# Three-pass output projections, and another order at the front of the last mixture, in a two-layer decoder on Trainium2

## The chip, the cores and the metric

The kernel runs on one core of one Trainium2 chip. The metric is device time in microseconds of one execution. "Before" and "after" mean the kernel without and with the change described below. Line numbers (L2137) are lines of the kernel before.

## The reference

The input x is (4, 512, 256) in float32; ctx has the same shape. Six sublayers follow each other, each as `x = x + sublayer(layernorm(x))`:

```
L0  attn   causal self-attention, 16 heads of 16, q and k scaled by a rope factor, y @ W_proj.T + b_proj
L0  xattn  gelu(x ctx^T) * (x ctx^T), times ctx
L0  ffn    mixture: 8 experts of width 512, top 2 by softmax of the two logits, plus a shared expert
L1  attn   full self-attention, 16 heads of 16, att_v @ W_out.T + b_out
L1  xattn  attention over ctx, softmax over the queries, @ Wo + bo
L1  ffn    mixture: 8 experts of width 1024, top 2, each weight a masked softmax (mask: (m - logit) / max(|logit|, m) > 0.02)
```

The change touches the output projections of both self-attentions and the last sublayer:

```
logits = x @ gate_w.T                    # 2048 tokens, 8 experts
routing_weights, selected = phi_routing(logits)   # two softmaxes over masked logits, one per choice
out += wte[:, e:e+1] * ((silu(x @ w1[e].T) * (x @ w3[e].T)) @ w2[e].T)
```

## The kernel before

Partitions are 128 rows. A batch is 512 tokens, four tiles (`NT`). Five programs run one after the other, with a barrier between them: `attention` for layer 0 (tag l0a: four causal batches), `geglu` (l0g), `moe` for layer 0 (l0m), `attention` for layer 1 (l1a: four self batches, then four cross batches) and `moe` for layer 1 (l1m). In each, a generator writes out one list of steps, and each engine walks that list in order and does the steps it has a part in. So the order of the list is the order of every engine's queue, and semaphores join them.

**Precision.** A plain fp32 matmul on TensorE is two records of the trace for each product. Where the kernel splits both operands into a rounded part (`hi`, float32r, made by ScalarE as a copy) and a rest (`lo`, by a subtraction on VectorE or GpSimd), `three_passes` multiplies hi by hi, lo by hi and hi by lo: three records. Before, the input projections of self batches from the second on and all products of the mixtures were done so; the output projection (`project`, step OUT, L1066 to L1074) was plain fp32.

**Attention.** The list runs in slots: a group of four heads (`g`) has eight slots (`j`), and a slot has scores by key (S), their exponential on ScalarE, in self batches the scores by query of a later group and their row maxima on VectorE (A), and between them the rest of the work. For an out-projection the outputs of two groups are turned back (N: `turn_back` on TensorE into `m_ps`, `copy_back` on ScalarE into `oT`). The projection of a batch comes one batch later: steps OUT at slots 4 and 7 of group 1 in self batches, and at slots 9 and 15 (counted through the batch) of the first cross batch. Each OUT does two token tiles with two halves of the heads each: four products of 128 by 128 by 256. VectorE adds the result to x (ADD). Score buffers form a ring of three. SPLIT rounds the q, k and v weights in the first slots (ScalarE, then GpSimd), XSPLIT does the same for the turned x.

**The mixtures.** Rows are sorted by expert into 23 blocks: 16 of 256 rows and 7 of 128. Each block has one set of weights, w13 in `NF` chunks (512 KB each; `NF` is 2 in l0m, 4 in l1m) and w2 (1 MB in l1m). The steps for block n and chunk f: W or C (w13 of a chunk split, ScalarE then VectorE), G (both hidden products on TensorE, SiLU on ScalarE, product on VectorE), H (hidden rows split), V or CV (w2 split), Y (output product), T (gathered rows turned by TensorE and split). GpSimd gathers the rows of block n + 2 once block n's are turned. In l1m there is one raw w13 buffer and one raw w2 buffer.

**The front of l1m**, in order: LN and TURN per batch; LOGITS; then on VectorE the routing, whose steps each wait for the one before: TOP1, TOP2; RANK (TensorE counts places); EXPERTS (blocks used and, at L2292 to L2299, which expert a block has: `block_expert`, then `experts_known`); ROWS and PLACES (L2341 to L2350, ends with `placed`); HELD (GpSimd writes tile and place of each token, four products, L1864); eight spot rows per step SPOT (VectorE, L2356) and their list products LIST (TensorE). Then UNMASKED 0 and EXP 0 (a masked softmax's differences), LISTS (the row list, `listed`), GATHER, C for chunk 0, UNMASKED 1, EXP 1, SHARES (12 steps for the weights in three parts), WEIGHTS (GpSimd, six products, L1871), TensorE kept warm with 24 idle matmuls, T of block 0, then C for chunk 1 and the first block's G, H and so on. LOAD on SyncE's queue waits for `experts_known` and issues the four chunks of block 0's w13. The space of raw w2 holds half of the spots, so w2 is loaded only after the weight lists (LIST part 2) were made, behind G of chunk 1. The first Y waits for w2's split and for the row weights (WEIGHED).

## Time and profile before

| | us |
|---|---|
| median of 3 runs | 1590.3 (1586.99 to 1592.11) |
| profiled execution | 1590.26 |
| its span, first to last instruction | 1588.5 |
| TensorE busy in the span | 1417.9 (89%) |
| VectorE busy | 1176.2 (74%) |
| ScalarE busy | 908.1 (57%) |
| GpSimd busy | 635.8 (40%) |

The engines are named PE (TensorE; PEld its weight loads), DVE (VectorE), ACT (ScalarE), POOL (GpSimd) and SP (SyncE, which only issues transfers here). The five programs lie at about 0 to 290 us (l0a), 290 to 360 (l0g), 360 to 645 (l0m), 645 to 1156 (l1a, cross batches from about 940 on) and 1156 to the end (l1m). Matmuls overlap, so one lasts longer than the distance to the next. PEclk is the clock granted to TensorE as a share of 2.4 GHz.

### The profile page before, as it was taken

Reading aid. Unit: us, or ns where it says so; the run is one execution under the profiler, and the core shown is the slowest. Engines: PE = TensorE matmul, PEld = TensorE weight load, DVE = VectorE, ACT = ScalarE, POOL = GpSimd, SP = SyncE. Lnnn points to the kernel's source line nnn. Section 1 sums busy time; section 2 is a strip of 40 time slices with the busy share of each in tenths; the row PEclk is TensorE's granted clock in tenths of the full one; section 3 lists DMA queues with packets and bytes.
Section 4 is the critical chain, followed back from the end, with each engine's and each line's share of the span. In section 5 each row is a group of like instructions: output and inputs, shape, how many; then the busy total and the mean of one; then the engine's idle time right before and its main releaser. Section 6 shows DMA issues by size and latency. Waiting matters only on the chain. (4 is left out here: it accounts for less than half of the span.)

```text
span 1588.5 us, 30443 instructions
## 1 busy us (share of the span) xinstructions
PE 1417.9 (89%) x10014; PEld 1000.2 (63%) x10014; DVE 1176.2 (74%) x2501; ACT 908.1 (57%) x1722; POOL 635.8 (40%) x899
## 2 busy tenths in 40 slices
PE   7899998989899999679999999898757899999997
PEld 3455554559899999424444433333245899999997
DVE  4777662554778888378788849998868688888885
ACT  1455553223256666136675678998813577766673
POOL 6565530010225665475554452553314233332221
PEclk8799998998999999869999999999987999999999
DMA  6223210220359887443223331332034687887882
GB/s 172 50 57 62 62 42 16 65 93 34 104 149 255 247 243 210 117 100 61 53 49 55 61 74 42 74 74 64 17 133 136 199 245 240 234 242 230 235 236 68
DMA packets 104571, 194.60 MB, mean 123 GB/s; under 512 B 30465, under 2 KB 55937, under 8 KB 101473
## 3 DMA queue, kind: packets, MB, share of 16 engines
q1 hardware_dynamic: 71760, 154.23, 31.2%
q0 software_dynamic: 31872, 37.79, 13.5%
q8 instruction: 80, 1.31, 0.3%
q10 hardware_dynamic: 784, 0.66, 0.1%
q14 instruction: 75, 0.61, 0.1%
HBM read 135.89 MB, written 18.61 MB: 97 GB/s over the span
## 5 line engine op out<-in xcount | busy, mean ns | idle before, releaser
L878 ACT ACTIVATE l1a_sb_probs<-l1a_s_ps,l1a_sb_kmax 128x512 f32<-128x512 f32 x256 | 172.5, 709 | 18.6 <-DVE l1a_sb_kmax L801 17.7
L766 DVE TENSOR_REDUCE l1a_sb_mx<-l1a_s_ps 128x2 f32<-128x1024 f32 x128 | 153.4, 1218 | 36.5 <-PE l1a_s_ps L982 36.4
L801 DVE TENSOR_REDUCE l1a_sb_kmax<-l1a_s_ps 128x1 f32<-128x512 f32 x256 | 160.5, 677 | 20.4 <-PE l1a_s_ps L1021 19.7
L884 ACT ACTIVATE l1a_sb_probs<-l1a_s_ps 128x1024 f32<-128x1024 f32 x128 | 130.1, 1024 | 72.6 <-PE l1a_s_ps L1021 72.0
L1021 PEld LDWEIGHTS l1a_s_ps<-l1a_sb_qst,l1a_sb_kst 49*128 49x128 f32 (+1 forms) x512 | 48.7, 189 | 163.8 <-issue 87.9
L761 DVE CUSTOM_DVE_ANT_0 l0a_sb_seen<-l0a_s_ps,l0a_sb_above 128x128 f32<-128x128 f32 (+3 forms) x256 | 113.5, 487 | 51.5 <-PE l0a_s_ps L982 51.2
L630 POOL DMA_DIRECT2D l1a_sb_kst<-l1a_sb_hi x228 | 112.8, 498 | 86.7 <-PE l1a_s_ps L1021 80.6
L2137 PE MATMUL l1m_g_ps<-l1m_sb_rows_hi,l1m_sb_hi 128*128 128x256 f32 x512 | 146.8, 287 | 0.4 <-DVE l1m_sb_late L2027 0.4
L2137 PE MATMUL l1m_g_ps<-l1m_sb_rows_lo,l1m_sb_hi 128*128 128x256 f32 x512 | 145.3, 284 | 0.0
L2137 PE MATMUL l1m_g_ps<-l1m_sb_rows_hi,l1m_sb_lo 128*128 128x256 f32 x512 | 145.3, 284 | 0.0
L1021 PE MATMUL l1a_s_ps<-l1a_sb_qst,l1a_sb_kst 49*128 49x512 f32 (+1 forms) x512 | 125.3, 498 | 21.4 <-ACT l1a_sb_probs L878 19.2
L2001 DVE TENSOR_TENSOR l1m_sb_lo<-l1m_sb_raw,l1m_sb_hi 128x512 fp32r<-128x512 f32 x184 | 119.3, 691 | 18.5 <-ACT l1m_sb_hi L1905 17.4
L1845 POOL DMA_INDIRECT out_x<-l1m_sb_late,l1m_sb_add_to x37 | 60.9, 1647 | 174.8 <-DVE l1m_sb_late L2049 165.0
L884 ACT ACTIVATE l0a_sb_probs<-l0a_s_ps 128x1024 f32<-128x1024 f32 (+3 forms) x128 | 88.8, 702 | 60.8 <-PE l0a_s_ps L991 60.3
L2137 PE MATMUL l0m_g_ps<-l0m_sb_rows_hi,l0m_sb_hi 128*128 128x256 f32 x384 | 113.1, 294 | 7.1 <-DVE l0m_sb_rows_lo L1995 6.4
L2137 PE MATMUL l0m_g_ps<-l0m_sb_rows_hi,l0m_sb_lo 128*128 128x256 f32 x384 | 111.1, 289 | 0.0
L2137 PE MATMUL l0m_g_ps<-l0m_sb_rows_lo,l0m_sb_hi 128*128 128x256 f32 x384 | 111.1, 289 | 0.0
L1905 ACT ACTIVATE l1m_sb_hi<-l1m_sb_raw 128x512 fp32r<-128x512 f32 x184 | 104.8, 621 | 0.0
L2137 PEld LDWEIGHTS l1m_g_ps<-l1m_sb_rows_hi,l1m_sb_hi 128*128 128x128 f32 x512 | 98.7, 193 | 1.2 <-issue 0.6
L2137 PEld LDWEIGHTS l1m_g_ps<-l1m_sb_rows_hi,l1m_sb_lo 128*128 128x128 f32 x512 | 98.7, 193 | 0.0
L2137 PEld LDWEIGHTS l1m_g_ps<-l1m_sb_rows_lo,l1m_sb_hi 128*128 128x128 f32 x512 | 98.6, 193 | 0.0
L2137 PE MATMUL l1m_y_ps<-l1m_sb_hi,l1m_sb_h_hi 128*128 128x256 f32 x312 | 90.3, 289 | 8.2 <-DVE l1m_sb_lo L2007 7.2
(437 smaller groups left out, 4011.5 us busy)
## 6 DMA issues: line engine op xcount, KB each, us to landing
l1m_sb_raw<-in_l1m_w SPq DMA_DIRECT2D x92, 512.0 KB, 4.6
l0m_sb_raw<-in_l0m_w SPq DMA_DIRECT2D x72, 512.0 KB, 4.8
l1m_sb_raw<-in_l1m_w SPq DMA_DIRECT2D x23, 1024.0 KB, 6.2
l1a_sb_qst<-l1a_sb_hi SPq DMA_DIRECT2D x256, 32.0 KB, 2.1
l1a_sb_kst<-l1a_sb_hi POOLq DMA_DIRECT2D x228, 32.0 KB, 2.0
l0a_sb_qst<-l0a_sb_hi SPq DMA_DIRECT2D x128, 32.0 KB, 2.2
l1a_sb_qst<-l1a_sb_lo SPq DMA_DIRECT2D x128, 32.0 KB, 2.1
l0a_sb_kst<-l0a_sb_hi POOLq DMA_DIRECT2D x124, 32.0 KB, 2.1
```

The costliest lines, as they stand in the source:

```text
L630: pool.dma_start(in_stack(kst, p, e, n), in_part(source, i, p, e)).then_inc(kstacked[p], 16)
L761: ins = dve.tensor_tensor_reduce(seen[:, j % 2, e, 0:last], buffer("A", b, g, j)[:, e, 0:last], above[:, T - last:T], 1.0, -3e38, ALU.add, ...
L766: dve.tensor_reduce(mx[:, g, qt, 2 * p:2 * p + 2], buffer("A", b, g, j)[:, :, :], AX.X, ALU.max).then_inc(a_max.sem, 1)
L801: dve.tensor_reduce(kmax[:, n % 4, e:e + 1], buffer("S", b, g, j)[:, e, :], AX.X, ALU.max, negate=True).then_inc(kmax_done.sem, 1)
L878: ins = act.activation(probs[:, n % 8, e, :], at[:, e, :], ACT.Exp, bias=kmax[:, n % 4, e:e + 1], accum_out=zsum[:, n % 4, e:e + 1])
L884: act.activation(probs[:, n % 8, :, c0:T], at[:, :, c0:T], ACT.Exp, scale=SCALE).then_inc(exp_done.sem, 1)
L1021: ins = pe.matmul(at[:, e, c0:T], kst[rows, p, kt * P:(kt + 1) * P], qst[rows, p, c0:T], start=True, stop=not causal)
L1845: pool.indirect_dma_start(total, bass.IndirectOffsetOnAxis(ap=at, axis=0), y[:, e % 2, t, :], None, compute_op=ALU.add).then_inc(stored[e ...
L1905: ins = act.activation(two_chunks(hi, s % 2, f), raw13[:, s % n13, f, n, :, :], ACT.Copy)
L2001: ins = dve.tensor_tensor(two_chunks(lo, s % 2, f), raw13[:, s % n13, f, n, :, :], two_chunks(hi, s % 2, f).bitcast(F32), ALU.subtract)
L2137: ins = pe.matmul(at, s, m, start=first and n == 0, stop=final and n == len(passes) - 1)
```

## The change

1. Output projections: in `attention`, `project` uses `three_passes` for the self batches that are not the last batch of the program (`out_parts`: three of l0a, four of l1a). A step OSPLIT comes one slot behind each N: ScalarE rounds `oT` into `o_hi`, GpSimd subtracts into `o_lo`, and `project` waits for it. A fourth SPLIT does the output weights. To make room, `o` takes the rope table's space in l1a and the cross batches' `ox` that of `oT`.
2. Both mixtures: of HELD's four products GpSimd keeps two; ScalarE does the other two as copies with a scale. ScalarE's and VectorE's shares of C and CV become steps of their own (CHI, CVHI).
3. l1m: another order from RANK to the second block. UNMASKED 0 comes right behind RANK, the `block_expert` part of EXPERTS (now BLOCKS) and LOAD behind the spots, SHARES and WEIGHTS behind T of block 0, chunk 1's split ahead of T. Half of the spots lie in x's space (VectorE first waits for the copy of x to memory, `summed`), so w2 is loaded in LOAD, which waits for the first gathered rows after two chunks of w13. w2's split and the second set's chunks move between the first two blocks' steps.

```diff
@@ attention schedule: self_slot and cross_slot (there at j == 7)
-        if first and nxt is not None and j < 3:
+        if first and nxt is not None and j < 4:
             yield "SPLIT", nxt, j, 0
@@
         if j == turn_at and has_last and last[1] % 2:
             yield "N", *last, 0
+        if j == turn_at + 1 and has_last and last[1] % 2:
+            yield "OSPLIT", *last, 0
@@ attention
+            def split_out(b, g, _):                         # GpSimd
+                pair = g // 2
+                if out_parts[b]:
+                    o_round.wait(pool, b, pair)
+                    pool.tensor_tensor(o_lo[:, pair, :], oT[:, pair, :], o_hi[:, pair, :].bitcast(F32), ALU.subtract
+                                       ).then_inc(o_rest.sem, 1)
+            def split_out(b, g, _):                         # ScalarE
+                pair = g // 2
+                if out_parts[b]:
+                    oT_copied.wait(act, b, pair)
+                    act.activation(o_hi[:, pair, :], oT[:, pair, :], ACT.Copy).then_inc(o_round.sem, 1)
@@ project
+                if out_parts[b]:
+                    if b == 0:
+                        pe.wait_ge(w_rest, 4)
+                    o_rest.wait(pe, b, pairs[-1])
...
+                    if out_parts[b]:
+                        ins = three_passes(m_ps[:, (t % 2) * D:(t % 2 + 1) * D],
+                                           [((o_hi[:, pair, rows], o_lo[:, pair, rows]),
+                                             (wout_hi[:, pair, :], wout_lo[:, pair, :])) for pair in pairs])
+                        continue
@@ moe_schedule, layer 1
-        for step in ("TOP1", "TOP2", "RANK", "EXPERTS", "LOAD", "ROWS", "PLACES", "HELD"):
+        for step in ("TOP1", "TOP2", "RANK", "UNMASKED", "EXP", "EXPERTS", "ROWS", "PLACES", "HELD"):
             yield step, 0, 0
         for c in range(NSPOT):
             yield "SPOT", c, 0
             yield "LIST", c, 1
-        yield "UNMASKED", 0, 0
-        yield "EXP", 0, 0
+        yield "BLOCKS", 0, 0
+        yield "LOAD", 0, 0
         yield "LISTS", 0, 0
         yield "GATHER", 0, 0
-        yield "C", 0, 0
         yield "UNMASKED", 1, 0
         yield "EXP", 1, 0
-        yield "SHARES", 0, 0
-        yield "WEIGHTS", 0, 0
+        yield "CHI", 0, 0
+        yield "C", 0, 0
+        yield "CHI", 0, 1
+        yield "C", 0, 1
 
         yield "IDLE", 24, 0
         yield "T", 0, 0
         yield "IDLE", 5, 0
-        yield "C", 0, 1
-
-        between = {1: [("LIST", c, 2) for c in range(NSPOT)] + [("WEIGHED", 0, 0)], nf: [("CV", 0, 0)]}
+        yield "SHARES", 0, 0
+        yield "WEIGHTS", 0, 0
+        yield "CHI", 0, 2
+        yield "C", 0, 2
+
+        between = {2: [("LIST", c, 2) for c in range(NSPOT)], 3: [("WEIGHED", 0, 0)]}
@@ weights_beside
         if nf > 2 and n == 0:
-            return (1, f - 1) if f else (1,)
+            return (1, 1) if f == nf - 1 else (1,)
+        if nf > 2 and n == 1:
+            return ((1, 2), (1, 3), (2, 0, 1), (2, 2, 3))[f]
@@ chunk
-        if nf > 2 and n == 1 and f == 0:
-            yield from prepared(1, nf - 1)
         yield "G", n, f
-        if nf > 2 and n == 0 and f < 2:
-            yield "C", 0, f + 2
+        if nf > 2 and n == 0 and f == 0:
+            yield "CHI", 0, 3
+            yield "C", 0, 3
+        if nf > 2 and n == 0 and 0 < f < 3:
+            for part in (2 * f - 2, 2 * f - 1):
+                yield "CVHI", 0, part
+                yield "CV", 0, part
...
+        if nf > 2 and n == 0 and f == 1:
+            yield from prepared(1, 0)
@@ moe
-                     for t in (raw2[:, 0, :, :].rearrange("p f d -> p (f d)"),
+                     for t in (x[:, 0:NTILE // 2, :].rearrange("p n d -> p (n d)"),
@@ LOAD on SyncE
                 for f in range(NF):
+                    if f == 2 and not shared:
+                        sp.wait_ge(rows_in[0], halves_to(0) * 16)
                     load_w13(s, e, f)
+                if not shared:
+                    load_w2(s, e)
@@ HELD: GpSimd keeps the first part, ScalarE has the second
+            def held_in_tile(*_):
+                act.wait_ge(placed, 1)
+                for k in range(TOP):
+                    act.activation(held[:, k, :, 1, :], own[:, k, :, :], ACT.Copy, scale=const["token"][:, 0:1]
+                                   ).then_inc(in_tile_held, 1)
@@ SPOT on VectorE
+        if c == 0 and phi:
+            dve.wait_ge(sems["summed"], 16)
```

## Rows read from the trace of the kernel before

**Rows 1.** Stages: start:end, length; busy us (records) per engine; clock, DMA share, GB/s.
```profile
985.00:1156.00 171.00, 145.99 (x790) 54.93 (x786) 152.07 (x310) 148.80 (x429) 77.16 (x161) 0.98 0.25 55
1156.00:1239.00 83.00, 49.77 (x448) 39.57 (x448) 63.77 (x196) 24.93 (x46) 23.32 (x27) 0.80 0.46 154
1239.00:1588.00 349.00, 336.65 (x2642) 328.48 (x2642) 274.90 (x446) 226.10 (x420) 99.22 (x69) 0.98 0.73 214
```
**Rows 2.** Waits of PE, 1211 to 1300: total us, times, longest us.
```profile
PE l1m_y_ps L2137 <- DVE l1m_sb_lo L2007: 7.2, 1, 7.2
```
**Rows 3.** Chain of waits, 1200 to 1300: start us, us, what.
```profile
1206.73 4.59 DMA l1m_sb_rows<-xn_dram,l1m_sb_take
...
1213.87 3.69 PE l1m_g_ps L2137 x24
...
1239.29 4.73 PE l1m_y_ps L2137 x24
1244.02 2.88 PE l1m_g_ps L2137 x24
```
**Rows 4.** Timeline of PE at an output step: start us, us, instructions.
```profile
783.09 1.97 PE L1073 MATMUL l1a_m_ps<-l1a_sb_wout,l1a_sb_oT 128*128 128x256 f32 x8
784.98 0.50 PE L1021 MATMUL l1a_s_ps<-l1a_sb_qst,l1a_sb_kst 49*128 49x512 f32 x2
```
**Rows 5.** All waits, 760 to 850: total us, times, longest us.
```profile
ACT l1a_sb_probs L884 <- PE l1a_s_ps L1021: 25.7, 28, 1.7
```
**Rows 6.** Lines L848 and L639: ns min/median/max, first and last start.
```profile
L848 ACT ACTIVATE l1a_sb_x_hi<-l1a_sb_xnT x6: 620/622/641, 705.3 to 831.4; 128x512 fp32r<-128x512 f32 x6
L639 POOL TENSOR_TENSOR l1a_sb_x_lo<-l1a_sb_xnT,l1a_sb_x_hi x6: 1272/1280/1286, 706.0 to 832.1; 128x512 fp32r<-128x512 f32 x6
```
**Rows 7.** Timeline of PE and ACT in the first cross group.
```profile
954.69 1.99 PE L1073 MATMUL l1a_m_ps<-l1a_sb_wout,l1a_sb_oT 128*128 128x256 f32 x8
...
958.09 0.76 ACT L878 ACTIVATE l1a_sb_probs<-l1a_s_ps,l1a_sb_kmax 128x512 f32<-128x512 f32 x1
```
**Rows 8.** Timeline of ACT and PE in layer 0's mixture.
```profile
414.33 0.60 ACT L1931 ACTIVATE l0m_sb_late<-l0m_g_ps 128x512 f32<-128x512 f32 x1 [3.77 <-PE l0m_g_ps L2137]
...
424.67 1.01 PE L2109 MATMUL l0m_t_ps<-l0m_sb_held,l0m_sb_spot 128*128 128x115 bf16 x16 [1.75 <-DVE l0m_sb_spot L2356]
```
**Rows 9.** Timeline of DVE at the front: RANK's wait, BLOCKS, ROWS, UNMASKED 0.
```profile
1182.35 0.17 DVE L2281 COPY l1m_sb_count<-l1m_t_ps 128x8 f32<-128x8 f32 x1 [1.69 <-PE l1m_t_ps L2092]
...
1184.58 0.73 DVE L2293 TENSOR_TENSOR l1m_sb_upto<-l1m_sb_end,const_iota 128x184 f32<-128x184 f32 x2
...
1186.46 0.17 DVE L2328 SCALAR_TENSOR_TENSOR l1m_sb_jump<-l1m_sb_end,l1m_sb_start 128x8 f32<-128x8 f32 x1
...
1201.37 0.28 DVE L2264 SCALAR_TENSOR_TENSOR l1m_sb_ab<-l1m_sb_lg 128x128 f32<-128x128 f32 x1
```
**Rows 10.** Timeline of POOL: the first of four held products.
```profile
1192.80 0.80 POOL L1864 TENSOR_TENSOR l1m_sb_held<-l1m_sb_own,const_iota 128x368 bf16<-128x368 bf16 x1 [25.53 <-DVEq L2349]
```
**Rows 11.** Spots (L2356) on DVE in two stretches: busy us (records), clock, DMA.
```profile
1192.90:1195.90 3.00, 2.98 (x5) 0.50 0.52 213
...
1198.30:1201.40 3.10, 3.10 (x17) 0.50 0.00 0
```
**Rows 12.** Line L1714, 1187 to 1226: time from issue to landing.
```profile
DMA to landing us min/median/max: 3.3/4.0/6.8
```
**Rows 13.** One stage more, with columns as in rows 1.
```profile
1229.00:1233.00 4.00, 3.10 (x27) 2.86 (x25) 2.95 (x5) 3.24 (x7) 0.62 (x1) 1.00 0.91 355
```
**Rows 14.** Timeline of DVE and POOL, 1205 to 1216: splits, SHARES, WEIGHTS.
```profile
1205.49 1.29 DVE L2001 TENSOR_TENSOR l1m_sb_lo<-l1m_sb_raw,l1m_sb_hi 128x512 fp32r<-128x512 f32 x2
...
1209.30 0.29 DVE L2306 TENSOR_TENSOR l1m_sb_df<-l1m_sb_df,l1m_sb_keep 128x128 f32<-128x128 f32 x1 [0.43 <-ACT l1m_sb_l L1888]
...
1212.42 5.51 POOL L1871 TENSOR_TENSOR l1m_sb_held<-l1m_sb_own,l1m_sb_share 128x368 bf16<-128x368 bf16 x6 [2.01 <-DVEq L2320]
...
1213.73 2.01 DVE L2001 TENSOR_TENSOR l1m_sb_lo<-l1m_sb_raw,l1m_sb_hi 128x512 fp32r<-128x512 f32 x2 [0.35 <-ACT l1m_sb_hi L1905]
```

More of the change, by code:

```diff
@@ L359, in attention @@
         probs = sb("probs", [P, 8, 2, T])
-        o = sb("o", [P, T])
+        o = const["rope"] if has_cross else sb("o", [P, T])
         rz = sb("rz", [P, NT, GH])
@@ L400, in attention @@
         w_round, w_rest = sem("w_round"), sem("w_rest")
+        out_parts = [b + 1 < NB and kinds[b] != "cross" for b in range(NB)]
+        o_round, o_rest = (Counts(sem(n), [2 if yes else 0 for yes in out_parts]) for n in ("o_round", "o_rest"))
         hi_done = steps("hi_done", 4)
@@ L1380, in moe_schedule @@
         for f in range(1, nf):
+            yield "CHI", 0, f
             yield "C", 0, f
-        yield "CV", 0, 0
+        for f in range(nf):
+            yield "CVHI", 0, f
+            yield "CV", 0, f
         yield "LN2", 3, 0
@@ L1389, in moe_schedule @@
                    4: [("RANK", 0, 0), ("UNMASKED", 0, 0)],
-                   5: [("EXP", 0, 0), ("EXPERTS", 0, 0), ("LOAD", 0, 0)],
+                   5: [("EXP", 0, 0), ("EXPERTS", 0, 0), ("BLOCKS", 0, 0), ("LOAD", 0, 0)],
                    6: [("SHARES", 0, 0), ("ROWS", 0, 0)],
@@ L1762, in next_w2 @@
                     load_w2(s, e)
-            def first_w2(*_):
-                if not shared:
-                    sp.wait_ge(weights_listed, 1)
-                    load_w2(0, expert(0))
             def second_w13(_, f):
@@ L1774, in second_w13, with second_w2 @@
                     load_w13(1, e, f)
-            def second_w2(*_):
-                if not shared:
+            def second_w2(_, f):
+                if not shared and f == NF - 1:
                     w2_done.wait(sp, 0, NF - 1)
@@ L1860, in held_tokens @@
                 tile_first = const["iota"][:, 32 + 3 * NBLK + 1:].unsqueeze(2).to_broadcast([P, NTILE, NBLK])
-                in_tile = const["token"][:, 0:1].unsqueeze(2).to_broadcast([P, NTILE, NBLK])
                 for k in range(TOP):
-                    for n, part in enumerate((tile_first, in_tile)):
-                        pool.tensor_tensor(held[:, k, :, n, :], own[:, k, :, :], part, ALU.mult).then_inc(tokens_held, 1)
+                    pool.tensor_tensor(held[:, k, :, 0, :], own[:, k, :, :], tile_first, ALU.mult).then_inc(tokens_held, 1)
             def held_weights(*_):
@@ L1913, in split_w2 @@
                                ACT.Copy).then_inc(w2_split.sem, 1)
-            def first_w2(*_):
-                for f in range(NF):
-                    split_w2(0, f)
             def next_w13(n, f):
@@ L1945, in end @@
                                   ).then_inc(const["x_back"][0], 16)
-            run({"END": end, "TURN": turned_rows, "EXP": exp, "T": rows_of, "C": split_w13, "CV": first_w2, "W": next_w13,
+            run({"END": end, "TURN": turned_rows, "HELD": held_in_tile, "EXP": exp, "T": rows_of, "CHI": split_w13, "CVHI": split_w2, "W": next_w13,
                  "V": next_w2, "G": gate, "H": split_h})
@@ L2009, in rest_w2 @@
                                   ).then_inc(w2_done.sem, 1)
-            def first_w2(*_):
-                for f in range(NF):
-                    rest_w2(0, f)
             def next_w13(n, f):
@@ L2058, in end @@
                                   ALU.mult).then_inc(end_read, 1)
-            run({"END": end, "LN1": ln, "LN2": normal, "T": rows_of, "C": rest_w13, "CV": first_w2,
+            run({"END": end, "LN1": ln, "LN2": normal, "T": rows_of, "C": rest_w13, "CV": rest_w2,
                  "W": next_w13, "V": next_w2, "G": hidden, "H": rest_h, "Y": output} | routing)
@@ L2291, in experts, with blocks @@
         then(dve.tensor_tensor(end, start, used, ALU.add))
+    def blocks(*_):
+        end = full("end")
         for k in range(2):
@@ L2382, in row_weights @@
         then(dve.tensor_tensor(full("row_weight"), full("row_weight"), at["row_holds"][:, :, 4, :], ALU.add))
-    return {"TOP1": top1, "TOP2": top2, "UNMASKED": unmasked, "EXPERTS": experts, "SHARES": shares, "ROWS": rows,
+    return {"TOP1": top1, "TOP2": top2, "UNMASKED": unmasked, "EXPERTS": experts, "BLOCKS": blocks, "SHARES": shares, "ROWS": rows,
             "PLACES": places, "SPOT": spot, "LISTS": lists,
```

30 lines of the change are left out of this document (21 added, 9 removed).

## The prediction

> **What bounds the kernel now.** Read first the table of stages [rows 1]. After 1239 TensorE is busy 336.65 of 349 us: it sets the time. It does not in layer 1's cross batches (985 to 1156: VectorE 152.07 and ScalarE 148.80 of 171, a ring of scores, maximum and exponential), and least of all from 1156 to 1239, the front of layer 1's mixture: TensorE 49.77 of 83 us, transfers 0.46. There I went to the waits of TensorE [rows 2]: one of 7.2 us, for VectorE's rest of w2. Third, the chain of waits [rows 3]: the first gathered rows land at 1211.33 (1206.73 + 4.59), the first block's passes stand in the chain from 1213.87, and its output product `Y` only at 1239.29. That product takes 4.73 us where the same 24 records take 2.88 later: after the idle gap it starts at the lower clock. From 1244 to the end the chain is TensorE almost throughout, so an earlier start there moves the end by as much.
>
> **Part A: output projections in three passes.** `out_parts` holds for three batches of layer 0 and four of layer 1, two steps each: 14 steps. A step was four fp32 products, recorded as 8 records, 1.89 us from its start to the next scores [rows 4]; it becomes 12 records, at the 0.120 us spacing of the mixture's three passes (2.88 / 24, [rows 3]) 1.44 us, with the same tail of about 0.19 us 1.63. Each step gives back 0.26 us. Bounds: nothing, where TensorE waits for another engine behind it, and 0.45, without the tail. The six of layer 0 and the first six of layer 1 lie where ScalarE and VectorE wait for TensorE (ScalarE 25.7 us in 28 waits in 90 us of layer 1's self batches, [rows 5]); I take 12 x 0.26 = -3.1.
>
> Added: 14 roundings on ScalarE, 0.62 us each, and 14 subtractions on GpSimd, 1.27 us each, by the same operations on x [rows 6]; one more of each per layer for the weights. In self batches they are queued six or more slots ahead of the product on engines that wait for TensorE there: nothing; if that cover went, a product would wait up to 1.9 us. The weight split falls between the x-bias addition and the splits of x on GpSimd; it pushes the first x rest by no more than its own 1.27 us, with a slot between that and the product that reads it: nothing.
>
> The cross slot is another matter: N is at slot 6, the split at 7, the product at 9. TensorE runs ahead of ScalarE: the product starts at 954.69, three slots before ScalarE's first exponential of slot 10 at 958.09 [rows 7]. Now ScalarE first ends slot 7's two exponentials (at 955.4, two slots of 1.33 us before 958.09), then the rounding (to 956.05), GpSimd the rest to 957.4, and only then TensorE. Behind the product on its queue stand slot 10's scores: 957.45 + 1.5 = 959.0, their maximum by 960.1, so ScalarE's exponential of slot 10 starts near 960.2 where it was 958.09. ScalarE and the ring are the bound here: +2.1 us, of which slack in the ring may absorb some; I take +1.9 (bounds 0.6, the rounding alone, and 3). The second product there (slot 15) hides its gain: 0.
>
> Part A: -3.1 + 1.9 = -1.2. Reusing the rope table and oT as storage adds no wait that isn't there (oT is read out by then through the same `out_ready`).
>
> **Part B: the first mixture (layer 0).** Its order is the same on every engine, except that two of the `held` products move from GpSimd to ScalarE. ScalarE now waits for `placed` in front of the SiLU that starts at 414.33 [rows 8], which VectorE reaches at about the same time; two copies of 368 elements, each below the 0.60 us that 512 take, put that SiLU near 415.4. TensorE has two blocks' products to run meanwhile. GpSimd is done 1.6 us sooner, and TensorE's 1.75 us wait for the first spots (424.67, [rows 8]) shrinks. Between +1 and -1.5; I take -0.5.
>
> **Part C: the front of layer 1's mixture.** Step by step to the gather:
> 1. VectorE waits 1.69 us for `ranked` [rows 9]; UNMASKED (six steps from 1201.37 on, 1.93 us) moves into that wait: +0.25 there.
> 2. BLOCKS (1184.58 to 1186.46, five steps, [rows 9]) leaves that chain: -1.88. It goes behind the spots, where UNMASKED stood, with the same length: 0 there.
> 3. While GpSimd makes `held` (four products of 0.80 us from 1192.80 on, [rows 10]), VectorE gets one spot through per product: 4 or 5 in 3.0 us, against 16 or 17 in 3.1 later [rows 11]. With two products left there, 1.5 us hold two spots and the other two take 0.4: -1.1 (bounds 0 and -2.2).
> So the gather starts 2.7 us sooner, and the rows land at 1208.6 if nothing is in their way.
>
> 4. The weights. LOAD hung on `experts_known` and was issued at 1187.40; now it hangs on BLOCKS, behind the spots: 1203.3 - 2.7 + 1.1 (the same lag from block_expert to issue) = 1201.7. Landings took 3.3 to 6.8, median 4.0 us [rows 12]: chunk 0 at 1205.7, chunk 1 near 1207. CHI and C of both (C 1.29 us each, [rows 14]) fill the gather's wait, done by 1209.3, after UNMASKED 1. First row split, ready at 1210.5: G(0,0) starts at 1210.6 instead of 1213.44, again at the lower clock. Chunks 2 and 3 and w2 wait for the gather and go out from 1208.7. At 512 KB in some 1.5 us (the transfers reached 355 GB/s averaged over 4 us, [rows 13]) they land near 1212.5, 1214 and 1217, set 1's first two near 1220.
> 5. SHARES (1209.30 to 1212.3, 3.0 us, [rows 14]) was free in the gather's wait; now it stands behind the row split, to 1213.6, and GpSimd's six WEIGHTS products (5.51 us) run beside C(0,2), C(0,3) and H(0,0). Two subtractions took 2.01 us instead of 1.29 beside them [rows 14] (0.72 more for the pair, nearly all of it on the second): between 0.36 and 0.72 for each of five or six, I take the upper end, 3.5 us.
> 6. VectorE in the new order then: C(0,2) to 1215.6, SiLU product 1216.3, C(0,3) 1218.9, H(0,0) 1219.8, T1 1220.5, G(0,1) 1221.2, half of w2 1222.4, H(0,1) 1223.0, W(1,0) 1224.3, G(0,2) 1224.9, the other half 1226.1, H(0,2) 1226.7, G(0,3) 1227.3, H(0,3) 1228.6, W(1,1) 1230.2, then the row weights at 1230.5.
> 7. TensorE: G(0,0) 1210.6 to 14.7, T1, G(0,1) to 18.0, G(0,2) to 20.9, the 64 list products to 23.0, G(0,3) to 25.9, G(1,0) to 28.8, T2, and Y(0,0) waits for the row weights: 1230.6. It takes 2.9 us, because the gap before it is 1.3 us and not 7.2. It ends at 1233.5 instead of 1244.02: -10.5. Of this 2.8 comes from the gather, 5.9 from the wait (7.2 to 1.3), 1.8 from the clock.
> 8. In block 1 both chunks W(2,0) and W(2,1) now lie between V and H(1,2): H(1,3) ends some 9.5 us after Y(0,1) instead of 8.5, and Y(1,0) wants it at 8.9: +0.6. After that both orders are the same and TensorE bounds.
> Part C: -9.9; bounds -4 (the first rival below) and -12.
>
> One rule of the Trainium skill (SBUF — State Buffer, Who interferes with whom) speaks against step 5: a VectorE instruction with two SBUF inputs and a GpSimd one that reads SBUF shut each other out for a whole instruction. By it each of six subtractions could lose a full product of 0.8 us, 4.8 in place of 3.5, and the sum would be -10.3; the 2.01 us row shows 0.72 for two of them, so I stay with the row.
>
> **Sum.** -1.2 - 0.5 - 9.9 = -11.6 on the profiled execution's own 1590.26 us (span 1588.5, 1.8 outside it), which equals the median of the runs, 1590.3. Forecast 1579.
>
> **Rivals.**
> *The weights come late (half the gain).* For: the first load moves by 14 us, from an idle stretch into the gather's; 1 MB at 355 GB/s is 3 us in front of the gather's own packets. The Trainium skill (DMA: Bandwidth & Descriptors, Issuing engines are not separate DMA queues) says that all issuers share the same 16 engines; no row here shows a gather beside 1 MB. Against: the gather is issued 0.9 us after the load and its second half 1.4 us later, and its rows are wanted later than the weights. Price: gather +3 and w2 at 1221 instead of 1217, which pushes VectorE's queue by 3: gain 5 to 6, 1585.
> *The wait of 7.2 us only changes its name.* Y(0,0) also waits for the row weights, whose products on GpSimd start at 1213.7 instead of 1212.42 and may be stretched to 1.25 us each, with TensorE's list products in front of G(0,3). If VectorE, locked out, runs 4 us later than in step 6: 1583.
> *Slower: the weight stream becomes the bound.* There are twenty-three sets of 3 MB. If TensorE after 1239 were fed by the stream with no slack, the stream's start 14 us later would reach the end: +14, less 2.8 (gather), less 1.7 (Parts A and B), 1600. It decides once a chunk lands later than its turn in block 1. Against: transfers are busy 0.73 there [rows 1], chunk loads wait for VectorE to free the one raw buffer, and by 1229 the stream owes 3.5 MB, some 12 us of work in 27.
> *No change.* The reordering is absorbed elsewhere and Part A costs what it gives: 1589.
>
> **How the numbers follow.** Forecast 0.68 (its own range 1575 to 1583); weights late 0.13; renamed wait 0.08; no change 0.07; slower 0.04. Of the two middle ones a sixth ends above 1585.5. A difference of 0.3%, 4.8 us, is what a measurement of this kernel tells from none. So faster 0.86, same 0.10, slower 0.04. Range 1574 to 1587: the lower end is Part C's bound of -12 with Part A's gains unspoilt, the upper one takes in both middle cases.
>
> **What would show it.** Step 1 to 3: the first gather near 1202.6, and spots of which only two are stretched. Step 4: no ScalarE wait for transfers before the row split. Step 7: Y(0,0) near 1230.6 without the 7.2 us wait and at 2.9 us. Part A: 12 records per step in 1.45 us, and one TensorE wait of 2 to 3 us near 955 in the first cross group. It is wrong if the passes before Y(0,0) wait for transfers, or if 1239 to the end (now 349 us after Y starts) grows.

## The result, and the profile after

| | us |
|---|---|
| after, median of 20 runs | 1584.28 (1578.56 to 1590.24) |
| before, median of 20 runs on the same chip | 1592.12 (1586.69 to 1603.27) |
| ratio after / before | 0.994, 95% interval 0.9924 to 0.9957 |
| profiled execution of after, and its span | 1583.6, 1581.7 |

The time lies inside the forecast's range (1574 to 1587). The ratio is worth 9.5 us of 1592 (6.8 to 12.1; the medians alone differ by 7.8), where 11.6 were forecast. It is the sum of a part that came as worked out and of one that did not. By stages of the two profiled executions (each starts with the first LayerNorm instruction of its program):

| stage | before | after | change | forecast |
|---|---|---|---|---|
| attention, layer 0 | 274.79 | 270.76 | -4.03 | -1.6 (six steps) |
| geglu and mixture, layer 0 | 382.22 | 382.16 | -0.06 | -0.5 |
| attention, layer 1 | 499.25 | 507.10 | +7.85 | +0.3 |
| mixture, layer 1 | 432.24 | 421.68 | -10.56 | -9.9 |

Stages of after, with the columns of [rows 1]: the cross batches, the front of the last mixture up to its first output product, and the rest.

```profile
985.00:1160.00 175.00, 153.54 (x778) 57.45 (x775) 150.20 (x307) 147.27 (x422) 76.77 (x160) 0.91 0.24 53
1160.00:1233.40 73.40, 49.38 (x448) 38.84 (x449) 59.08 (x186) 23.20 (x42) 21.74 (x24) 0.81 0.47 162
1233.40:1581.00 347.60, 335.31 (x2642) 326.90 (x2642) 280.09 (x455) 229.00 (x426) 100.10 (x70) 0.99 0.74 217
```

The first output product starts 73.4 us into the mixture, where [rows 3] has 83.0 (1239.29 less 1156.26), and the rest is 347.6 us. The other thing to see is the clock of the first line, 0.91 where [rows 1] has 0.98: the cross batches lost what the front gained.

**The front of the last mixture.** The chain of waits of after, 1195 to 1260 (start us, us, what), answers to [rows 3]:

```profile
1195.25 4.27 DVE x_sb L2412 x16
...
1208.90 1.41 issue
1210.31 2.56 DVE l1m_sb_lo L2055 x4
1212.87 0.61 DVE l1m_sb_rows_lo L2049
1213.53 3.14 PE l1m_g_ps L2188 x24
...
1231.98 1.45 issue
1233.42 3.10 PE l1m_y_ps L2188 x24
```

The wait of 7.2 us [rows 2] is gone, and what stands at its place is 1.45 us ("issue" is a wait for which the profile names no engine; 1.3 were forecast, for the row weights). VectorE's timeline (1232.5 to 1234) shows that it is the row weights: the copy of the weight lists out of the tile that the output product overwrites ends at 1233.27, 0.15 us ahead of that product.

```profile
1232.97 0.30 DVE L2435 COPY l1m_sb_row_holds<-l1m_y_ps 128x138 f32<-128x138 f32 x1
```

The waits of TensorE, 1204 to 1300 (total us, times, longest):

```profile
PE l1m_y_ps L2188 <- issue: 1.9, 2, 1.4
PE l1m_g_ps L2188 <- DVE l1m_sb_rows_lo L2049: 0.8, 1, 0.8
```

**The attention.** An output step of a self batch in after, on TensorE's timeline:

```profile
785.41 0.39 PE L948 MATMUL l1a_m_ps<-l1a_sb_wout_hi,l1a_sb_o_hi 128*128 128x256 f32 x1
...
786.82 0.28 PE L948 MATMUL l1a_m_ps<-l1a_sb_wout_lo,l1a_sb_o_hi 128*128 128x256 f32 x1
787.03 0.50 PE L1050 MATMUL l1a_s_ps<-l1a_sb_qst,l1a_sb_kst 49*128 49x512 f32 x2
```

From its start to the next scores it is 1.62 us where [rows 4] shows 1.89. The first output step among the cross batches, and the scores that follow it:

```profile
948.03 0.49 PE L1050 MATMUL l1a_s_ps<-l1a_sb_qst,l1a_sb_kst 48*128 48x512 f32 x2
951.59 0.36 PE L948 MATMUL l1a_m_ps<-l1a_sb_wout_hi,l1a_sb_o_hi 128*128 128x256 f32 x1 [3.06 <-POOL l1a_sb_o_lo L657]
...
953.72 0.79 PE L1050 MATMUL l1a_s_ps<-l1a_sb_qst,l1a_sb_kst 48*128 48x512 f32 x2
```

The wait stands where the forecast put it, 3.06 us long. The splits cost what [rows 6] said (ns minimum, median, maximum; first and last start):

```profile
L873 ACT ACTIVATE l1a_sb_o_hi<-l1a_sb_oT x8: 622/622/674, 742.1 to 949.5; 128x512 fp32r<-128x512 f32 x8
L657 POOL TENSOR_TENSOR l1a_sb_o_lo<-l1a_sb_oT,l1a_sb_o_hi x8: 1264/1285/1306, 742.8 to 950.2; 128x512 fp32r<-128x512 f32 x8
```

Following VectorE's additions to x through both traces, layer 1's 7.85 us fall into pieces: +0.9 at its very start (a stacked key arrives late: TensorE waits 2.6 us for a transfer before the fourth of its first products), -1.95 over the six self steps, +2.55 at the first cross step, +2.6 and +2.65 at the next two borders of cross batches, +0.8 at the last, and small ones. The two pieces in the middle are the clock's. Two stretches of after, then the same work in before (columns as above):

```profile
996.00:1007.00 11.00, 11.00 (x44) 3.90 (x38) 7.85 (x17) 9.73 (x29) 5.90 (x10) 0.54 0.44 110
1051.00:1062.00 11.00, 11.00 (x46) 4.29 (x39) 7.86 (x16) 9.73 (x28) 5.46 (x10) 0.53 0.43 103
```

```profile
999.00:1010.00 11.00, 9.46 (x60) 4.24 (x56) 8.97 (x18) 11.00 (x32) 6.84 (x14) 1.00 0.43 109
1053.00:1064.00 11.00, 9.63 (x59) 3.96 (x52) 9.00 (x19) 10.81 (x33) 5.56 (x13) 1.00 0.37 89
```

At 0.54 (nearly all of it at the lower level, 1.2 GHz) TensorE is busy without a gap and gets 44 records done in 11 us. At 1.00 it gets 60 done and has time over. In the first case it, and no longer the ring of ScalarE and VectorE, sets the pace.

### The profile page after: what moved, and what is told of

It is laid out like the page before. It is cut to its first block and busy times, and to the rows that moved or that the text cites. A ratio compares the mean times of both kernels' runs of the same rounds, so it can differ in the third digit from the quotient of the medians.

```text
span 1581.7 us, 30588 instructions
## 1 busy us (share of the span) xinstructions
PE 1420.8 (90%) x10070; PEld 1002.1 (63%) x10070; DVE 1175.9 (74%) x2501; ACT 918.5 (58%) x1742; POOL 650.5 (41%) x911
## 5 line engine op out<-in xcount | busy, mean ns | idle before, releaser
L1050 PE MATMUL l1a_s_ps<-l1a_sb_qst,l1a_sb_kst 49*128 49x512 f32 (+1 forms) x512 | 128.8, 510 | 18.8 <-ACT l1a_sb_probs L907 16.2
```

What stands on the lines that cost most here:

```text
L1050: ins = pe.matmul(at[:, e, c0:T], kst[rows, p, kt * P:(kt + 1) * P], qst[rows, p, c0:T], start=True, stop=not causal)
```

## The experiments

Beside after's own 20 runs, they ran in three sets on three chips: attn_only, moe_only, no_cross and weights_early; after_again, wait_only, cross_wide and best1; double_s and the last three. Each set shares runs of before on its chip; before's mean clock was 0.9470, 0.9470 and 0.9466 on the three, so they can be laid side by side. The row of before has the 59 runs of these three sets; the 20 beside after's own runs have no clocks on record. Times are medians over the runs of each. "Lower clock" counts the us between 900 and 1170 in the profiled execution in which TensorE had the lower level.

| kernel | runs | median us | ratio to before (95%) | attention L1 | lower clock | mean clock of all runs |
|---|---|---|---|---|---|---|
| before | 59 | 1594.6 to 1596.7 | | 499.25 | 14 | 0.9469 |
| after | 20 | 1584.28 | 0.994 (0.9924 to 0.9957) | 507.10 | 38 | 0.9463 |
| moe_only | 12 | 1582.35 | 0.9927 (0.9900 to 0.9955) | 505.72 | 27 | 0.9493 |
| attn_only | 12 | 1595.3 | 1.0004 (0.9977 to 1.0031) | 503.12 | 20 | 0.9435 |
| after_again | 8 | 1582.28 | 0.9921 (0.9891 to 0.9951) | 506.88 | 34 | 0.9469 |
| wait_only | 7 | 1583.27 | 0.9939 (0.9912 to 0.9965) | 499.80 | 14 | 0.9466 |
| cross_wide | 6 | 1581.16 | 0.9917 (0.9894 to 0.9941) | 505.94 | 38 | 0.9465 |
| weights_early | 12 | 1583.21 | 0.9919 (0.9893 to 0.9946) | 506.30 | 27 | 0.9473 |
| no_cross | 6 | 1573.67 | 0.9887 (0.9839 to 0.9936) | 496.03 | 10 | 0.9518 |
| best1 | 4 | 1574.09 | 0.9883 (0.9854 to 0.9912) | 495.98 | 10 | 0.9512 |
| double_s | 11 | 1582.83 | 0.9924 (0.9894 to 0.9954) | 502.81 | 14 | 0.9512 |

The same code takes 499.25 us (before) and 505.72 us (moe_only) for layer 1's attention, so one execution's clock can hide a change of this size. The three kernels with one run each at the end of this section have after's attention too: 506.98 (w2_late), 503.60 (shares_early) and 506.39 us (held_pool). Over all executions of a kernel its time falls by 1.09 us for each 0.001 of mean clock (slope fitted within the kernels, the scatter around it about 2 us). Moved with it to one mean clock of 0.948, the kernels take: before 1594.0, attn_only 1590.4, moe_only 1585.0, after 1582.8, wait_only 1582.1, weights_early 1582.2, after_again 1581.3, no_cross 1580.2, cross_wide 1579.8, best1 1578.3, double_s 1586.7, each to 0.3 to 0.9. That splits a difference into the order's own part and the clock's, but not cleanly: a shorter wait in the front of the last mixture also takes time at the lower clock away. Between 1155 and 1245 TensorE had the lower level for 37.5 us in before and for 27.3 in after. So a part of the mixtures' own gain is counted as the clock's.

**attn_only and moe_only: each part alone.** The first has the attention's functions of after and the mixtures' of before, the second the reverse.

> The kernel before with the attention part alone (three-pass output projections); both mixtures as before. In the profiled runs layer 0's attention took 4.0 us less after the change and layer 1's 7.8 us more; of the 7.8, 2.6 lie at the first cross slot's wait for GpSimd's rest and 5.3 in two stretches (996 to 1007, 1052 to 1063) in which TensorE was granted the lower clock. Theory 1, the lower clock follows from the change (the wait shifts TensorE against ScalarE, and the gaps fall otherwise): it is there again, layer 1's attention takes 505 to 508 us, the kernel is 1 to 4 us slower than before. Theory 2, the two falls are of that execution alone: layer 1's attention takes 499.3 - 2.0 (six steps of 0.33) + 2.6 + about 1 = 500 to 502, layer 0's gains 1.9 to 2.2, and the kernel is 0 to 2 us faster than before.

> The kernel before with the two mixtures' part alone; attention as before. Both theories: the last mixture takes 421 to 423 us instead of 432.2, layer 0's changes by less than 0.7, and the kernel takes about 1579.5 where before takes 1590.3 (ratio 0.993). Rival: the gain of the last mixture was partly the state in which attention leaves the chip (its clock): then it is under 8 us.

The attention's part alone makes no difference that can be told (-3.7 to +4.9 us), the mixtures' part gives 11.7 us (7 to 16). At one clock they give 3.6 and 9.0, together 12.6; after itself gives 11.2. Against theory 1, moe_only, which has the attention of before, also fell to the lower clock at 1008 and 1062, so the falls need no split. Against theory 2, attn_only has both falls, shorter (3.4 us each, at 1002 and 1057). Its layer 1 took 503.1 us, between the ranges of the two theories, and its time doesn't tell them apart. But the mean clock of its 12 runs is 0.0034 below before's (standard error of the difference 0.001), 3.7 us by the slope. So whether a fall comes varies between executions, but how much time is spent at the lower clock differs between kernels. The last mixture took 420.2 us in moe_only and 430.0 in attn_only: its gain stays with its own part. Layer 0's geglu and mixture took 385.1 us in moe_only, 2.9 more than in before, where less than 0.7 either way was expected; the other profiles with this part lie at 382.1 to 383.6, so one profile doesn't settle a change of this size.

after_again, the same kernel profiled once more, took 506.88 us for layer 1's attention. Both falls are there, the first of them 3.4 us long instead of 10.3. Over all profiles, a fall stands at the second border (1048 to 1073) in each of the eight with rounding, subtraction and passes in the cross batches (double_s, below, left aside), and at the first (996 to 1012) in six of them; of the four without, moe_only alone has any.

**no_cross: no split in the cross batches.**

```diff
-        out_parts = [b + 1 < NB and kinds[b] != "cross" for b in range(NB)]
+        out_parts = [b + 1 < NB and kinds[b + 1] != "cross" and kinds[b] != "cross" for b in range(NB)]
```

> The kernel after with the last self batch of layer 1 left out of out_parts, so that the two output steps in the first cross batch are plain fp32 and do not wait for GpSimd. Theory 1 (the clock's falls come from that wait): the wait of 3.1 us and both falls are gone, layer 1's attention takes 497.5 to 499, the kernel 1575 to 1577 where after takes 1583.6. Theory 2 (the falls are chance): 2.6 us less than after on the average, 1581, and the lower clock may still show in the cross batches.

The median is 1573.67, faster than either theory had it; the mean of the six runs is 1576.1, since two of them, at the clocks 0.944 and 0.947, took 1586.0 and 1579.7. It is 9.5 us by median and 6.9 by mean below weights_early on the same chip, whose attention is after's. Layer 1's attention took 496.0 us, less than the 497.5 to 499 of theory 1. The wait is gone, both falls are absent, no_cross and best1 stand 3.0 us below the two sets of after at one clock (1579.4 against 1582.4), and the mean clock of no_cross and best1 is 0.9516 over 10 runs against 0.9467 over the 53 runs of the five kernels that split or wait there and have the mixtures of after (difference 0.0049, standard error 0.0013): some 5 us more. moe_only, with the mixtures of after and no split at all, lies between them at 0.9493: 0.0027 above the 53 (standard error 0.0011), and not to be told from no_cross and best1 (0.0023, standard error 0.0017). Measured from it the clock's share is 3 us.

**wait_only and cross_wide: the wait without the passes, the passes without the wait.**

```diff
@@ wait_only: project
-                    if out_parts[b]:
+                    if out_parts[b] and kinds[b + 1] != "cross":
                         ins = three_passes(...
@@ cross_wide: cross_slot (N and OSPLIT each one slot earlier too)
-    outs = {9: (b - 1, 0, 0), 15: (b - 1, 0, 1)} if ...
+    outs = {10: (b - 1, 0, 0), 15: (b - 1, 0, 1)} if ...
```

> The kernel after, but the two output steps in the first cross batch are plain fp32 products of oT again, which still wait for GpSimd's rest of oT (rounded and subtracted as in after). The wait is kept, the three passes there are taken away. If the wait is what costs: as after, within 1 us (median near 1584), mean clock as after's 0.946. If it is the passes or the shorter busy stretch of TensorE: as the kernel without both (1574 to 1577).

> The kernel after with more room in the first cross batch: N one slot earlier (5), OSPLIT behind it (6), and the first output step one slot later (10 instead of 9); three passes kept. Two slots of 1.33 us against a wait of 3.1: the wait shrinks to 0.4 to 0.8 us. If the wait is what costs, by itself and by the clock behind it: most of the 8 us between after and the kernel without the split there come back, 1575 to 1578. Rival: an output step at slot 10 stands right ahead of the product of slot 12 and its wait only moves there: 1582 to 1584.

TensorE's waits in the first cross group (935 to 975), wait_only and then cross_wide:

```profile
PE l1a_m_ps L1112 <- POOL l1a_sb_o_lo L657: 3.0, 1, 3.0
PE l1a_o_ps L1084 <- ACT const_rope L920: 2.3, 1, 2.3
PE l1a_m_ps L1112 <- DVE l1a_sb_lo L760: 1.3, 1, 1.3
```

```profile
PE l1a_o_ps L1084 <- ACT const_rope L920: 2.3, 1, 2.3
PE l1a_m_ps L985 <- DVE x_sb L813: 1.4, 2, 0.8
PE l1a_m_ps L948 <- DVE l1a_sb_lo L760: 1.3, 1, 1.3
```

Two slots hide the wait wholly, and at one clock that is worth 1.5 to 3 us (1579.8 against after's 1582.8 and 1581.3), about the size of the piece at the first cross step. cross_wide's median of 1581.16 lies between the two ranges that were expected, because the mean clock stays at 0.9465, and the falls near 1000 and 1056 are in its profile. wait_only has the wait and not the passes; its median and its mean clock are after's, as expected for the case that the wait is what costs, while its one profile has no falls. At the first cross step wait_only loses 1.8 us against before, and 3.2 against no_cross, which gains 1.4 there. So the wait costs 2 to 3 us by itself, and neither it nor the passes are needed for the low mean clock: theory 1 is out. That either of them is enough alone is not excluded. What after, wait_only and cross_wide share is the work of the split itself, on ScalarE and GpSimd among the cross slots.

**double_s: do TensorE's gaps at a batch border set off the falls?**

```diff
-                for e in range(2):
+                border = cross and ((g == 3 and j >= 4) or (g == 0 and j < 2 and kinds[b - 1] == "cross"))
+                for e in (0, 1, 0, 1) if border else (0, 1):
```

> The kernel after, with each score product made twice (same data, same place, so the result does not change) in the last four slots of a cross batch and in the first two of the next: 0.43 us more of TensorE in each of six slots, where TensorE stood idle 0.6 to 0.75 us before three of the products. Three profiled runs of this attention fell to the lower clock at 996 to 1008 and at 1050 to 1066. If TensorE's gaps at the border of two cross batches set off those falls: both are gone, layer 1's attention takes 500 to 503 us instead of 507, the mean clock rises by 0.003 to 0.005. If the falls come whatever TensorE does there: they are there, and the doubled products cost 0 to 1.3 us per border on the ring of scores: 507 to 511 us.

TensorE's timeline ahead of the first fall, in after and at the same place in double_s:

```profile
994.16 0.50 PE L1050 MATMUL l1a_s_ps<-l1a_sb_qst,l1a_sb_kst 48*128 48x512 f32 x2 [0.69 <-ACT l1a_sb_probs L907]
995.41 0.51 PE L1050 MATMUL l1a_s_ps<-l1a_sb_qst,l1a_sb_kst 48*128 48x512 f32 x2 [0.75 <-ACT l1a_sb_probs L907]
```

```profile
999.39 0.73 PE L1051 MATMUL l1a_s_ps<-l1a_sb_qst,l1a_sb_kst 48*128 48x512 f32 x4 [0.46 <-ACT l1a_sb_probs L907]
1000.64 0.50 PE L1051 MATMUL l1a_s_ps<-l1a_sb_qst,l1a_sb_kst 48*128 48x512 f32 x2 [0.52 <-ACT l1a_sb_probs L907]
```

The two gaps alone do not make a fall. They are as long ahead of the same products in before, where none followed (timeline of TensorE, 994 to 999), and in wait_only and no_cross (0.69 and 0.74 us), which have none either:

```profile
996.30 0.50 PE L1021 MATMUL l1a_s_ps<-l1a_sb_qst,l1a_sb_kst 48*128 48x512 f32 x2 [0.69 <-ACT l1a_sb_probs L878]
997.55 0.50 PE L1021 MATMUL l1a_s_ps<-l1a_sb_qst,l1a_sb_kst 48*128 48x512 f32 x2 [0.75 <-ACT l1a_sb_probs L878]
```

The same 11 us stretches in double_s:

```profile
1001.00:1012.00 11.00, 9.47 (x58) 4.05 (x60) 8.83 (x19) 11.00 (x34) 6.86 (x13) 1.00 0.40 105
1056.00:1067.00 11.00, 9.65 (x60) 3.88 (x60) 8.83 (x18) 10.80 (x32) 5.42 (x12) 1.00 0.32 73
```

Both falls are gone, and a third one that every other profile had between 1094 and 1124. The attention takes 502.8 us, and the mean clock of 11 runs is 0.9512 against 0.9465 in the 28 of after (difference 0.0047, standard error 0.0008). The added products cost as much as the clock gave back (1586.7 at one clock, 4.3 more than the 28 runs of after), so nothing is won. One profile without falls would show little, since wait_only has one too; the mean over 11 runs is what speaks: work in TensorE's gaps at the borders, and no change elsewhere, keeps the clock up.

**weights_early and best1: the weights ahead of the spots.** BLOCKS and LOAD stand between HELD and the spots, and LOAD waits for nothing but BLOCKS. best1 adds no_cross's edit, and ScalarE's roundings ahead of UNMASKED 1.

```diff
-        for step in ("TOP1", "TOP2", "RANK", "UNMASKED", "EXP", "EXPERTS", "ROWS", "PLACES", "HELD"):
+        for step in ("TOP1", "TOP2", "RANK", "UNMASKED", "EXP", "EXPERTS", "ROWS", "PLACES", "HELD", "BLOCKS", "LOAD"):
@@ first_loads on SyncE
-                    if f == 2 and not shared:
-                        sp.wait_ge(rows_in[0], halves_to(0) * 16)
```

> The kernel after with BLOCKS and LOAD between HELD and the spots, and without LOAD's wait for the gathered rows: the first 3 MB of weights are issued near 1197.5 instead of 1205.4 to 1212. My theory: BLOCKS takes the place of spots in the 1.56 us in which GpSimd makes held, so the spots (4.27 us for the first 16) lose about 1.1 less, the gather starts 1.1 earlier, VectorE's idle 1.4 us before the first chunk's rest and ScalarE's 1.79 and 0.35 us waits for transfers go; Y(0,0) starts 1 to 2 us earlier, 1582. Rival: 3 MB of transfers stand in front of the gather's packets, rows land 1 to 2 us later, and nothing is gained or 1 us lost (1583.6 to 1585).

> Three edits of after together: no split in the cross batches; BLOCKS and LOAD behind HELD, without LOAD's wait; and ScalarE's rounding of the first two chunks ahead of UNMASKED 1, so that VectorE's 1.47 us wait for it goes. VectorE bounds from the spots to the first block (it is idle 1.5 us there), so the first two edits alone give nothing there and the third at most the 1.47, of which TensorE's 24 idle matmuls and the gathered rows' landing leave some 0.5. Against the kernel without the split in the cross batches (1573.7 in six runs, 1580.2 when moved to the common mean clock): 0 to 1.5 us less, 1572 to 1576.

The landmarks of the front, in us from the last mixture's start in the profiled execution (gather: the first indirect transfer on GpSimd):

| kernel | gather | first hidden product | first output product | whole mixture |
|---|---|---|---|---|
| before | 49.05 | 57.18 | 83.03 | 432.24 |
| attn_only | 49.05 | 56.92 | 83.31 | 429.99 |
| after | 46.38 | 53.51 | 73.40 | 421.68 |
| moe_only | 46.38 | 53.52 | 73.45 | 420.16 |
| no_cross | 46.37 | 53.52 | 73.43 | 420.90 |
| weights_early | 47.33 | 54.47 | 74.39 | 420.79 |
| best1 | 47.35 | 54.24 | 74.11 | 420.68 |
| held_pool | 47.52 | 54.63 | 75.25 | 423.44 |
| shares_early | 46.38 | 56.63 | 77.91 | 425.70 |
| w2_late | 46.39 | 53.51 | 85.09 | 434.18 |

My theory for weights_early was wrong. The five BLOCKS steps in GpSimd's shadow were stretched themselves: two of them took 1.76 instead of 0.72 us, which is what two spots lose there in after (1.53 for 0.48). And where they had stood they covered VectorE's wait for the last list product, now 0.89 us, so the gather starts 1 us later, not 1.1 earlier. The whole mixture takes no longer for it. best1 is 0.3 us quicker to its first output product than weights_early. It and no_cross are the fastest kernels of the study, 1.1 to 1.2% below before, not to be told apart by time.

**w2_late, shares_early, held_pool: the front's terms one by one.** Each undoes one edit of after. Each has a single run, so only places within the front are read from it, and not its time.

```diff
@@ w2_late: LOAD has no w2; SyncE at WEIGHED; no CVHI and CV in block 0
+            def listed_w2(*_):
+                if not shared:
+                    sp.wait_ge(weights_listed, 1)
+                    load_w2(0, expert(0))
+        between = {..., nf: [(step, 0, part) for part in range(nf) for step in ("CVHI", "CV")]}
@@ shares_early: SHARES and WEIGHTS from behind T to behind C 0, 1
         yield "C", 0, 1
+        yield "SHARES", 0, 0
+        yield "WEIGHTS", 0, 0
@@ held_pool: GpSimd's four products again, none on ScalarE
+                    for n, part in enumerate((tile_first, in_tile)):
+                        pool.tensor_tensor(held[:, k, :, n, :], own[:, k, :, :], part, ALU.mult)
```

> The kernel after, but the first w2 is loaded only once the weight lists are made (as in before), and its split stands behind the second block's first chunk. All else in the front of the last mixture as after. My largest term was that TensorE's 7.2 us wait for w2's rest goes (5.9 of the 9.9 us). Then here: w2 is issued near 1226 instead of 1212 (run after's times), lands 5 to 7 us later, 8 split instructions follow, and the first output product starts 3 to 7 us later, at +76.5 to +80.5 from the mixture's start instead of +73.4; the mixture takes 424 to 428 us instead of 420.9. Rival (the row weights bound it as well): less than 1.5 us later.

> The kernel after, but SHARES and WEIGHTS stand behind the split of chunk 1, ahead of T of the first block, as they did in before. My step 5 said the move behind the row split makes room for the first block: with SHARES (3.0 us) back in front, the first hidden product starts 1.6 to 3.0 us later than +53.5 from the mixture's start (VectorE had 1.4 us idle there, but not at the place of SHARES). The first output product starts 0 to 2 us later than +73.4, since VectorE does the same work up to it. Rival, contention decides: GpSimd's six products then run earlier, beside VectorE's idle time, the splits are not stretched (3.5 us in my sum), and the output product starts 1 to 3 us earlier.

> The kernel after, but all four held products on GpSimd again (ScalarE does none), in both mixtures. My step 3 and part B: the gather starts 1.1 us later (bounds 0 and 2.2) than +46.38 from the last mixture's start, the first output product as much later than +73.4; layer 0's mixture with geglu takes 0.5 us more (-1 to +1.5) than 382.2. Rival: ScalarE's copies disturb VectorE as GpSimd's products did, and nothing changes.

In w2_late TensorE waits again, longer than in before. Its wait, then the transfer that the chain names for it:

```profile
PE l1m_y_ps L2188 <- DVE l1m_sb_lo L2061: 13.1, 1, 13.1
```

```profile
1238.52 7.45 DMA l1m_sb_raw<-in_l1m_w
```

The output product starts 11.7 us later, more than the 3 to 7 expected, and the mixture takes 434.2 us (424 to 428 expected), 1.9 more than in before. The weight lists are made no later than in before (65.8 against 66.7 us from the mixture's start). What is late is the issue, at 74.4 us where before has 70.1: SyncE's queue has a w13 chunk ahead of w2, and the chain of waits shows it held until VectorE ends the split of an earlier chunk at 1237.24. The transfer then lands 7.5 us after it is issued, and the split behind it adds 3.2. So w2_late shows that w2 on time is what removed the wait, but its 11.7 us are more than the term. In shares_early the wait for the first rows grows to 4.0 us, and behind it the first hidden product runs at the lower clock:

```profile
1216.13 5.31 PE l1m_g_ps L2188 x24
```

5.31 us in place of 3.14 in after: 3.1 us of delay (1.6 to 3.0 expected) became 4.5 at the output product, above the 0 to 2 expected; and GpSimd's six products took 5.50 us instead of 6.85, so the contention did go away and was worth less than the delay. In held_pool the first 16 spots took 5.39 us instead of 4.27 and the gather started 1.14 us later; the forecast had 1.1. The first output product came 1.85 us later, not 1.1, behind a wait of 2.1 us where after has 1.45. The gather's place alone would not show a change of this size, since double_s, which has after's front, has its gather at 47.40. The spots do show it: the first 16 take 4.27 us in every profile with ScalarE's copies and this order, and 5.39 or 5.40 in the three without the copies. ScalarE's copies do not disturb VectorE. Layer 0's two stages took 382.33 us beside after's 382.16: part B is worth nothing there.

## Why the prediction was right in one part and wrong in the other

**Part C was right in its mechanism, and near in most of its terms.** Gather 2.67 us sooner (forecast 2.7), first hidden product 3.67 (2.84, and at the higher clock where I had the lower: VectorE was ready 0.8 us behind the turned rows, so TensorE's gap was 0.8 us), output product 9.63 (8.7), its length 3.10 where [rows 3] has 4.73. Block 1 gave 1.2 back (0.6), which leaves 10.1. The -10.56 of the table holds some of the clock of the rest as well: moe_only is 10.0 us ahead at the same place and 12.1 at the end. Undone singly, w2 is the largest of the three, and the spots lose the 1.1 us of HELD again. The rival of late weights did not come: ScalarE found the first two chunks landed and waited 1.79 and 0.35 us for the other two, while VectorE was still at SHARES.

Step 5's contention lay within its bounds. GpSimd's products and VectorE's subtractions in after, timeline of 1216.4 to 1223.5:

```profile
1216.54 6.85 POOL L1921 TENSOR_TENSOR l1m_sb_held<-l1m_sb_own,l1m_sb_share 128x368 bf16<-128x368 bf16 x6 [2.21 <-DVEq L2374]
1216.55 2.55 DVE L2055 TENSOR_TENSOR l1m_sb_lo<-l1m_sb_raw,l1m_sb_hi 128x512 fp32r<-128x512 f32 x2
...
1219.62 1.90 DVE L2055 TENSOR_TENSOR l1m_sb_lo<-l1m_sb_raw,l1m_sb_hi 128x512 fp32r<-128x512 f32 x2
...
1221.45 1.28 DVE L2083 TENSOR_TENSOR l1m_sb_h_lo<-l1m_sb_late,l1m_sb_h_hi 128x512 fp32r<-128x512 f32 x1
```

Of the splits beside GpSimd's six products the first pair took 2.55 us where 1.29 is undisturbed, the second 1.90, one rest of the hidden rows 1.28 instead of 0.68: 2.5 in all, where I had taken 3.5 (the times of step 6 hold only 2.3 of them: 0.72, 1.31 and 0.22), while GpSimd's own products took 6.85 instead of 5.51. The page of the Trainium skill weighed there (SBUF — State Buffer, Who interferes with whom) has the two shut each other out for a whole instruction. The trace agrees: each of the five subtractions ends 0.54 or 0.55 us behind the end of a product, and each later product 0.66 or 0.67 behind the end of a subtraction. What was wrong is the 4.8 that I had worked out from it, a full product for each of six: four subtractions lost 0.60 to 0.67, and one, which came as a product was ending, nothing.

**Part A was wrong, in one step.** The passes themselves gave 0.27 to 0.33 us a step (0.26), and the splits in the self batches cost nothing. The step that failed is "the cross slot is another matter": I priced it as a wait in the ring, +1.9. With what stands behind it, it cost 2.55, the clock at the lower level from 952.5 on included. With that the terms that I had sum to -1.3 (-1.9, -1.95 and +2.55), near the -1.2 forecast. But the split costs another 3 to 5 us through TensorE's clock, which no term of mine held: I took the 0.98 of [rows 1] for a property of the stage, when it was one execution's. With the split there, the mean clock is 0.9463 to 0.9473; without it 0.9493 (moe_only) and 0.9516 (no_cross and best1). So part A is worth nothing in time that can be told (-3.6 us at one clock), and without its last batch 5 us at one clock and 8.7 between the medians of no_cross and moe_only (7.5 between the means, with a standard error of about 2.6).

Layer 0's -4.0 is 1.9 of steps and 2.1 of the clock in its last 30 us (0.86 before, 0.98 after); its first stage varied from 270.8 to 279.7 us over profiles with the same attention, so these 2.1 are not the change's.

That the total lies in the range is luck in part. The clock's share, which the sum left out, was 3 to 5 us, and the range was wide enough for it only because Part C's gain came whole.

**Left open:** what in the split's work takes the clock down. Neither the wait nor the passes are needed for it, though either might be enough; moe_only has the falls with no split at all; and the gaps ahead of the first fall are as long where no fall follows. A version whose only addition is the rounding or the subtraction in the cross slots was not run.

## What to carry to other kernels

Price work that is put into a stretch twice: by the ring it delays, and by TensorE's mean clock over many executions with and without it. Before a clock row of a stage is used as a term, see how far it moves between executions of the same code; if time follows mean clock from run to run, compare kernels at one mean clock and the clock by itself. An edit that gives a fraction of a microsecond per step is to be applied where the engine it relieves is the bound, and not in the stretch where another one is: here leaving out one batch of seven was worth about as much as the other six together.

## What the runs showed of the hardware

- Where TensorE's clock fell at the first border of two cross batches, it did so 0.4 to 1.4 us after gaps of 0.69 and 0.75 us, with no longer gap close before (after, after_again, moe_only, attn_only), and it stayed at the lower level for 3.4 to 10.3 us, although TensorE was then busy without a break (11.00 of 11 us in after). The same gaps were not followed by a fall in before, wait_only, no_cross and best1. Filling part of them (0.46 and 0.52 left) raised the mean clock of 11 executions by 0.0047.
- The same attention code had these falls in one execution and not in another: 505.72 us in moe_only and 499.25 in before.
- VectorE and GpSimd took turns, instruction by instruction, where VectorE's subtractions met GpSimd's products. What a VectorE instruction lost went by the product and not by its own length: 0.60 to 0.67 us for a subtraction of 0.68 us, 1.04 us for two steps of BLOCKS (1.76 for 0.72), 1.05 us for two spots (1.53 for 0.48).
